# Self attention's sums from its exponentials' accumulated output, turned once by TensorE

## The reference, cut to what matters

```python
scores = jnp.einsum('bhid,bhjd->bhij', Q, K) / jnp.sqrt(jnp.asarray(d, q.dtype))
scores = scores + jnp.einsum('bhid,ijd->bhij', Q, rel_emb)
attn = jax.nn.softmax(scores, axis=-1)
ctx = jnp.einsum('bhij,bhjd->bhid', attn, V)
ctx = ctx.transpose(0, 2, 1, 3).reshape(b, s, e)
return ctx @ Wo + bo
```

## Time and profile before

| | us |
|---|---|
| median of three runs | 760.44 |
| lowest, highest | 759.88, 760.55 |
| the profiled execution | 758.19 |
| its span, first to last instruction | 756.4 |
| PE busy | 675.0 (89%) |
| DVE busy | 551.8 (73%) |
| ACT busy | 404.5 (53%) |
| POOL busy | 207.3 (27%) |

### The profile page before, as it was taken

One profiled execution on the slowest core, in us unless ns is written; L12 is line 12 of the kernel. 1 busy time (PEld: TensorE's weight loads), 2 busy tenths in 40 slices (PEclk: granted clock), 3 DMA queues, 4 the chain that ended last, 5 costly groups with the idle time before them and its releaser, 6 DMA issues.

```text
span 756.4 us, 21349 instructions
## 1 busy us (share of the span) xinstructions
PE 675.0 (89%) x8334; PEld 519.1 (69%) x8334; DVE 551.8 (73%) x2013; ACT 404.5 (53%) x1172; POOL 207.3 (27%) x213
## 2 busy tenths in 40 slices
PE   5888999999999999999878988899899989999886
PEld 2445777777777787777766976666666666666664
DVE  1236778888888888987647557888888788888853
ACT  3756666666766666663210224555555555555542
POOL 5312233333333315423344112222222222222100
PEclk9969999999999999999879999999999999999999
DMA  9776435555444455630032110000000011111000
GB/s 345 271 257 205 162 130 172 171 171 170 166 160 124 123 172 178 231 147 20 20 103 69 33 32 9 10 11 13 13 16 13 13 14 14 15 13 13 5 6 7
DMA packets 48259, 72.22 MB, mean 95 GB/s; under 512 B 2832, under 2 KB 43280, under 8 KB 45472
## 3 DMA queue, kind: packets, MB, share of 16 engines
q1 hardware_dynamic: 45120, 61.80, 24.3%
q0 software_dynamic: 2320, 5.18, 3.3%
q10 hardware_dynamic: 720, 3.88, 1.3%
HBM read 32.38 MB, written 38.47 MB: 94 GB/s over the span
## 4 chain that ended last, share of the span: by engine, by line
PE 58%; DVE 22%; issue 8%; ACT 7%; DMA 2%; another core or an unknown queue 1%; POOL 1%; SPq 0%; DVEq 0%; ACTq 0%
PE bank L560 49%; PE bank L621 4%; PE bank L706 3%; DVE k L1663 3%; DVE scol L1705 2%; ACT kbd L1210 1%; ACT kbd L1211 1%; DMA xT_ld<-xT 1%; DVE k L1641 1%; DVE kbd L1755 1%; DVE q L1732 1%; DVE y_d L1679 1%; ACT pTb L1105 1%; DVE stats_e L1313 1%
## 5 line engine op out<-in xcount | busy, mean ns | idle before, releaser
L1066 ACT ACTIVATE sc<-sc,nmxa 128x128 f32<-128x128 f32 x256 | 79.9, 393 | 34.9 <-DVE nmxa L1290 34.9
L499 POOL TENSOR_TENSOR early<-early,recb 128x616 f32<-128x616 f32 x32 | 38.9, 1216 | 187.6 <-DVE recb L1378 187.6
L1290 DVE CUSTOM_DVE_ANT_0 sc<-bank,rel 128x128 f32<-128x128 f32 x256 | 56.4, 286 | 14.7 <-PE bank L560 14.5
L1663 DVE TENSOR_TENSOR k<-bank,k_sb 128x512 f32<-128x512 f32 x64 | 41.2, 685 | 28.6 <-PE bank L560 23.7
L1300 DVE COPY pTa<-bank 128x512 f32<-128x512 f32 x32 | 22.0, 690 | 32.7 <-PE bank L621 32.7
L1046 ACT ACTIVATE rext<-bank 128x512 f32<-128x512 f32 x64 | 34.8, 609 | 18.2 <-PE bank L560 18.2
L476 POOL TENSOR_TENSOR rext<-rext,ones 128x1008 f32<-128x1008 f32 x16 | 29.9, 1868 | 52.7 <-ACT rext L1046 52.7
L560 PE MATMUL bank<-k,xdT 128*128 128x512 f32 x96 | 43.8, 592 | 0.0
L535 POOL TENSOR_TENSOR oTb<-x_all,row_sb 128x128 f32<-128x128 f32 x16 | 7.3, 457 | 132.9 <-DVE pTa L1684 132.9
L1113 ACT ACTIVATE early<-early 128x308 f32<-128x308 f32 x64 | 27.4, 454 | 29.4 <-DVE early L1363 29.4
L621 PE MATMUL bank<-k_sb,sc 128*128 128x128 f32 x256 | 36.4, 288 | 7.3 <-issue 6.5
(11 more groups left out here) (275 smaller groups left out, 1839.3 us busy)
## 6 DMA issues: line engine op xcount, KB each, us to landing
rel_dram<-rext SPq DMA_DIRECT2D x16, 2040.0 KB, 7.3
rel<-rel_dram SPq DMA_DIRECT2D x16, 960.0 KB
rext<-w_up SPq DMA_DIRECT2D x1, 1792.0 KB, 9.4
rel<-w_down SPq DMA_DIRECT2D x1, 1792.0 KB, 7.7
wb<-w_b ACTq DMA_DIRECT2D x1, 1604.0 KB, 16.5
xT_ld<-xT SPq DMA_DIRECT2D x16, 64.0 KB, 7.3
x_all<-x ACTq DMA_DIRECT2D x1, 1024.0 KB, 11.8
rel<-rel_dram SPq DMA_DIRECT2D x16, 64.0 KB
```

What stands on the lines that cost most here:

```text
L499: G.tensor_tensor(pB[:, part, :], pB[:, part, :], recb[:, part].unsqueeze(2).broadcast_to([P, 8, C]), ALU.mult).then_inc(b_even, 1)
L1066: last = A.activation(sc[:, h, :], sc[:, h, :], ACT.Exp, bias=nmxa[:, h:h + 1], scale=-1.0)
L1290: last = V.tensor_tensor_reduce(out=sc[:, h, :], in0=bank[i][:, a * P:(a + 1) * P], in1=rel[:, t % 2, h, :], scale=-1.0, scalar=FAR, op0=A ...
L1663: V.tensor_tensor(scd[:, 4 * i:4 * i + 4, :], bank[(1, 2, 0, 1)[i]][:].rearrange("p (a t) -> p a t", a=4), const("causal").unsqueeze(1).br ...
```

## The change

PE no longer forms the sums. Each exponential writes its row sum as accumulated output into `suma` (128 queries by 16 heads). A new step on DVE, `a_rec`, placed just ahead of `a_t3` in every order, inverts them, repeated eight times each, into `reca` (128x128). `a_values` starts with one transpose of `reca` into the columns where the sums stood and leaves `head_sums` out. ACT's step `a_v` becomes one copy from bank 0 to `rba` in place of logarithm and exponential. `recips["a"]` now counts two steps for each sequence.

```diff
@@ ORDER1 and TAIL1: "a_rec" ahead of every "a_t3" of the dve lists @@
-    "dve": ("a_t3 b_t1:-2 b_t3:-2 a_m0:1 ...
+    "dve": ("a_rec a_t3 b_t1:-2 b_t3:-2 a_m0:1 ...
...
+        suma = sb("suma", [P, H])
+        reca = sb("reca", [P, P])
...
@@ a_values @@
                 pe.wait_ge(a_pT_act, 2 * t + 2)
                 pe.wait_ge(a_pT_dve, 2 * t + 2)
-                head_products(bank[0], va[t % 3], pTa, P)
-                head_sums(bank[0], pTa, P).then_inc(values["a"], 1)
+                pe.wait_ge(recips["a"], 2 * t + 1)
+                pe.transpose(bank[0][:, P:2 * P], reca[:], ident)
+                head_products(bank[0], va[t % 3], pTa, P).then_inc(values["a"], 1)
...
@@ a_exp @@
                     act.wait_ge(maxed["a"], 4 * t + i + 1)
+                    if i == 0:
+                        need(act, recips["a"], 2 * t - 1)
                     for h in range(4 * i, 4 * i + 4):
-                        last = A.activation(sc[:, h, :], sc[:, h, :], ACT.Exp, bias=nmxa[:, h:h + 1], scale=-1.0)
+                        last = A.activation(sc[:, h, :], sc[:, h, :], ACT.Exp, bias=nmxa[:, h:h + 1], scale=-1.0,
+                                            accum_out=suma[:, h:h + 1])
...
+            def a_turned_recips(t):
+                act.wait_ge(values["a"], t + 1)
+                A.activation(rba[:], bank[0][:, P:2 * P], ACT.Copy).then_inc(recips["a"], 1)
...
-                "a_t0": a_turn(0), "a_t2": a_turn(2), "a_v": head_recips("a", 0, rba[:]), "a_ln": deviation("a"),
+                "a_t0": a_turn(0), "a_t2": a_turn(2), "a_v": a_turned_recips, "a_ln": deviation("a"),
...
+            def a_rec(t):
+                dve.wait_ge(exped["a"], 4 * t + 4)
+                need(dve, recips["a"], 2 * t)
+                V.reciprocal(reca[:].rearrange("p (h d) -> p h d", d=DH), suma[:].unsqueeze(2).broadcast_to([P, H, DH])).then_inc(recips["a"], 1)
+
-            def divide(k, b, rec, dst):
-                def f(t):
-                    dve.wait_ge(recips[k], t + 1)
+            def divide(k, b, rec, dst, steps=1):
+                def f(t):
+                    dve.wait_ge(recips[k], steps * (t + 1))
```

More of the change, by code:

```diff
@@ L124 @@
             "a_m1:13 v0:9 b_t1:9 a_st:12 r_b:11 a_t1:14 r_a:7 a_m1:12 b_st:11 a_m1:14 a_m0:13 b_rec1:10 r_c:10 "
-            "a_t1:12 b_u0:11 r_rows:8 b_u1:11 b_ag:10 a_t3:12 r_w:6 b_norm:8").split(),
+            "a_t1:12 b_u0:11 r_rows:8 b_u1:11 b_ag:10 a_rec:12 a_t3:12 r_w:6 b_norm:8").split(),
     "act": ("b_e0:12 b_t2:9 b_t2:10 b_e3:14 b_e3:10 b_t0:14 a_e3:12 b_qlo:10 a_t2:15 a_e0:12 a_qkv:15 a_t2:12 "
@@ L628, in head_products @@
                     for s in range(4):
-                        mm(ps[strip(s), 0:P], v[0:nk, s, 32 * a:32 * a + 32], pT[0:nk, 4 * s + a, :],
-                           start=(a == 0), stop=(a == 3))
+                        last = mm(ps[strip(s), 0:P], v[0:nk, s, 32 * a:32 * a + 32], pT[0:nk, 4 * s + a, :],
+                                  start=(a == 0), stop=(a == 3))
+                return last
             def head_sums(ps, pT, nk):
@@ L1546, in _ @@
                 "a_qkv": a_kv_, "rel_last": rel_last, "a_m0": a_max(0), "a_m1": a_max(1), "a_t1": a_turn(1),
-                "a_t3": a_turn(3), "a_div": divide("a", 0, rba[:], oTa[:]),
+                "a_t3": a_turn(3), "a_div": divide("a", 0, rba[:], oTa[:], 2), "a_rec": a_rec,
                 "a_add": add("a", 1, lambda t: x_all[:, t, :]), "a_st": stats_("a"), "a_ag": moments("a"), "a_ln": a_norm,
```

## The result

| | before | after |
|---|---|---|
| median (lowest to highest), us | 760.16 (758.17 to 760.55, 4 runs) | 749.44 (748.63 to 751.72, 4 runs) |
| the profiled execution, its span | 758.19, 756.4 | 751.72, 749.9 |

The account below looks back on a forecast made before the run. PE was taken to set the pace in a middle round. Thirteen rounds at 0.45 us gave 5.9, less 0.7 for the router, 5.2 us: profiled 758.19 to 753.0, median 755.2 us, range 753 to 759.

Parts of the forecast that it names:

- The handovers: Three lie close behind PE in a middle round; `b_s0` waiting for ACT's `b_qlo` would take 0.39 us.
- The read's price: On ACT, each exponential's accumulated output adds 0.106 us to its start-to-start distance, now 0.294 us.
- The transpose: On PE, one added turn of `reca` a round, taken as 0.14 us.
- PE's 0.85 as the gain of the free read: PE by itself gains 0.99 - 0.14 = 0.85 us a round, all of it counting if accumulated outputs cost almost nothing.
- The slack that I added up: DVE's 0.55 us of waiting at `b_m0` plus 0.31 at `b_out` just allows PE's whole 0.85 a round.
- the read is free: Faster rival: accumulated outputs add 0.01 us per exponential on ACT, PE's whole 0.85 counts, 750.1 us; chance 0.14.
- The reciprocal: DVE's `a_rec` between two `pTa` copies takes 0.87 us, hidden in a middle round.
- My term for the two router rounds: Where router batches end, 0.8 us of reciprocal on DVE exceeds its cover by 0.35; two places, -0.7 us.
- 13 x 0.45: First stage: 15 rounds less the router's two, each gaining 0.45 us, 5.9 us in all.
- the gap ahead of the turns: PE's only idle time in the middle of the first stage, 2.6 us in five rounds, 0.52 each.

Follow-up runs that it names:

- the shifted kernel before: Sixteen tiny products that nobody reads put ahead of all PE work in the kernel before; 754.12 us, ratio 1.004 (1.0014 to 1.0066).

## Why the prediction was right in sign and short in size

- *The handovers*: right. `b_s0` behind `b_qlo` became the wait, as the sum had it, though of 0.17 us (0.25 by start times) and not 0.39; putting the copy first removed it, lengthening ACT's work stretched it.
- *The read's price*: taken 0.106 us, measured 0.09. The nearest row on the same engine was the right one; DVE's hidden read was a poor guide. The round gained 0.52 against 0.45. The difference is 4 x 0.016 = 0.06 within a hundredth.
- *The transpose*: 0.20 us by start times in place of 0.14. PE's own saving is so 0.79 and not 0.85; since ACT set the start of `b_s0`, it changed only the wait.
- *PE's 0.85 as the gain of the free read*: wrong. Three kernels stop at 18.92, 0.66 under before. The slack that I added up, 0.55 on DVE plus 0.31 at `b_out`, passed over `b_v1`, which needs `b_l2`. This would have put the rival "the read is free" too low in time; the forecast didn't hang on it.
- *The reciprocal*: 0.944 us against 0.87, hidden in a middle round as said (without the read and without the sums the round is the same 18.92). The estimate from the Trainium skill's page "VectorE: DVE Perf Modes", section "First, the fixed hardware budget", was 1.2 us; the measurement lies between, nearer to the rows. In the router's rounds, 11 and 12, the kernel without the read is 0.50 and 0.68 us longer than the one without the sums, and in the last two rounds 0.56 and 0.79: 2.5 in all. That all of this is the reciprocal is not shown, since moving it shortened only rounds 12 and 15. My term for the two router rounds, -0.35 each, was a balance with PE's saving at nothing there. The balance measured is +0.05 for round 11 (20.07 without a stall, in the shifted kernel before, against 20.02) and -0.27 for round 12, so the term was too large. The last two rounds lost 0.54 together, where I had counted a gain of 0.9.
- *The start*: not in the sum. The first division is 1.6 us later, where ACT's exponentials are on the path and the reads cost 2.3 to 3.5. Rounds 1 and 2 lose 0.56 and 1.03, and this goes with the granted clock there: at the granted clock of before (0.90 and 1.00) the changed kernel with sixteen tiny products ahead gains 0.36 and 0.51 in them. I had read a middle round and no early one.
- *The step that failed* is the sum "13 x 0.45": it took thirteen rounds as alike, and the stalls of the kernel before as nothing. Rounds 4 to 9 and 13 gained 4.26, 0.61 each. But rounds 3, 10 and 11 gained 6.0, since the kernel before had stalls in them that went with the removed instructions. In the forecast these three stood for 2 x 0.45 - 0.35 = 0.55, as round 11 is a router round. What the stalls cost can be read off: round 3 is 22.39 with one and 19.33 in the shifted kernel without, round 11 is 21.18 and 20.07, round 10 is 20.45 and a plain one 19.58. That is 5.0 of the 6.0 us. I read the chain's share "issue 8%" and took it for the gap ahead of the turns, 0.52 a round, without looking whether all of it lay there. The row `rba` with its first and last start gave 19.5 us a round as a mean, below the middle round's 19.58 though three rounds of it were over 21, and I never laid the single distances side by side.

The parts, forecast and measured between the profiled executions:

| us gained | forecast | measured |
|---|---|---|
| up to the first division | 0 | -1.57 |
| rounds 1 and 2 | 0.9 | -1.59 |
| rounds 3, 10 and 11 (stalled in before) | 0.55 | 6.04 |
| rounds 4 to 9 and 13 | 3.15 | 4.26 |
| round 12 | -0.35 | -0.27 |
| rounds 14 and 15 | 0.9 | -0.54 |
| sum | 5.2 | 6.3 |

So the forecast's 5.2 lies close to the 6.5 us of the profiled pair by luck: 5.5 us too little in the stalled rounds was offset by 5.5 too much at both ends. What made the first set's medians differ by 10.7 is not shown by any profile.

The version that looks best is the changed kernel with the query copy first: ratio 0.9862, against 0.9917 for the changed kernel in a later set on the same chip. The two intervals overlap (one reaches up to 0.9907, the other begins at 0.9889), so that it beats the changed kernel rests on the profiles: from the first division to the sixteenth it is 279.8 us, against 284.6 and 284.3 in the two of the changed kernel. Moving the reciprocal as well measured the same, 0.9857 on another chip.

## What to carry to other kernels

Before a gain is multiplied by the number of rounds, write down the length of every round; those that stand out have a cause of their own, and an edit can remove or move it. Count the instructions that a change takes from or adds to a dense engine, apart from the time that they take there: here sixteen eight-column products cost 0.03 us in a middle round and, by the median, all of the gain in the total. Look at the granted clock round by round as well before a longer round is put down to an engine. When a stage loses its longest waits, look for the handover with the next smaller slack, one by one along the order, for it caps the gain.

## What the runs showed of the hardware

- An accumulated output on ScalarE is a separate record of 191 ns behind each activation, and lengthens a row of 128x128 exponentials from 0.294 to 0.384 us each by start times, 31%.
- A reciprocal on VectorE takes 243 ns for 128x16 and 944 for 128x128, 6.3 ns a column, and does not stretch beside POOL's operation of 1.87 us, where a copy of 227 ns from one tile to another took 1526.
- TensorE stood still for 0.36 to 1.53 us inside rows of short products without a wait that the profile names, in kernels that differ from stall-free ones by 32 records a round, and in three of the four kernels with such stalls the clock fell to 1.2 GHz behind the first of them. In the fourth, stalls of 0.36 and 1.07 us were not followed by a fall.
